# One layer of a post-norm decoder on one core: attention loads the turned x that the recurrence wrote to DRAM

## The chip, the core and the metric

The kernel runs on one core of a Trainium2 chip. The metric is the device time of one execution in microseconds (us). The core has a matrix engine (TensorE, PE in the profile, with its weight loads as PEld), VectorE (DVE), ScalarE (ACT), GpSimd (POOL) and SyncE (SP), which here issues every DMA. Engines run their own instruction streams in order and meet at semaphores.

## The reference, cut to what matters

Three layers follow each other, each with a residual and a layer norm behind it: a gated recurrence, a cross attention with `ctx_1024` as keys and values, and a quantised feed-forward. The batch is 64, the sequence 128, the width 256, with 16 heads of 16, all in float32.

```python
def _L0_attn_ref(x, Wq, Wk, Wv, Wf, bf, Wg, Wout, gamma, beta):
    q = (x @ Wq).reshape(b, s, H, HD)      # k and v alike
    fg = jax.nn.sigmoid(x @ Wf + bf).reshape(b, s, H, HD)
    ...
    def step(state, inp):
        qt, kt, vt, gt = inp
        state = state * gt[..., None] + vt[..., None] * kt[..., None, :]
        out_t = jnp.einsum('bhij,bhj->bhi', state, qt)
        return (state, out_t)
    ...
    out = (out - mu) * jax.lax.rsqrt(var + EPS) * gamma + beta
    out = out * jax.nn.silu(x @ Wg)
    return out @ Wout
...
x = _layernorm(x + _L0_attn_ref(x, ...), axis=-1)
x = _layernorm(x + _L0_xattn_ref(x, ctx_1024, ctx_1024, ...), axis=-1)
x = _layernorm(x + _L0_ffn_ref(x, ...), axis=-1)
```

x is a factor of two kinds of products: q, k, v and f of the recurrence, and the gate `x @ Wg`, which is computed later. Both need x with its features on the partitions, that is, x turned.

## The kernel before

The program is three blocks, one behind the other with a barrier between them: `recurrence_block` (L73), `attention_block` (L759) and `feedforward_block` (L1406). The first two work on pairs of batch rows, 32 pairs (`NP`) of 2 x 128 tokens. Despite its name the attention block also finishes the first layer: it loads the raw output of the recurrence, normalises it, multiplies it with the gate, applies `Wout`, adds x, and then does the cross attention.

**Recurrence.** Each engine runs a list of steps; in step p the front of pair p and the back of pair p-1 are done. SP's list is `load` (L196, the x of a pair: one DMA of 128 KB for the first batch row and four of 32 KB for the second, whose four chunks of 32 tokens are placed in reverse order) and `store` (L202, the output of a pair, one and four DMAs in the same way). Its loop (L232 to L236) runs over i = 2j+u: wait until pair i+1 has been turned, load pair i+3, wait until the output of pair i is ready, store pair i. An output is ready late: the back of pair i is done in step i+1, and its last sums, `total` on DVE (L712) and `gather` on POOL (L284), fall in step i+2. So `store(p-2)` is issued in the middle of step p, and `load(p+2)` directly behind it, since its own wait has long been met.

PE turns x with four transposes (`turn`, L326) into the PSUM bank F[0], and ACT copies the bank to `xT` (`turned`, L517). `xT` has one buffer of 128 x 2 x 256 float32 (256 KB). In step p, after the uses of exponent bank k = 1, ACT writes the turned x of pair p+1 (L547, L548); behind that copy on ACT stand the other uses of the exponents (L545), and PE waits for it in `value_gate(p+1, 0)` (L338), behind which stand the rest of the step's matmuls.

**Attention.** In a step PE, ACT, DVE and POOL work on four pairs at once (`old`, `prev`, `now`, `next_`). PE's order is written out in `step` (L1034). There x is loaded again from the input (`load`, L863), turned again by PE in `turn_x` (L912) through bank F[0] and copied by ACT in `x_out` (L1085) to the attention's own `xT`. Its reader is `gate` (L928). `turn_maxima` (L982) uses bank F[0] as well and therefore waits for the copy of x (`p.turned`), as does the first `turn_x1` (L946). The untransposed x in `xs` is needed for the residual too (L1299). The attention holds its batch rows in natural order.

**Feed-forward.** It is not touched.

Of the kernel before, what the change touches and what calls it, by code (L numbers as in the profile page):

```python
# [69 lines left out]

def recurrence_block(nc, t, w, x_d, o_d):  # L73

# [24 lines left out]
    with ExitStack() as ctx:  # L101
# [6 lines left out]
        def bank(name):  # L108
# [51 lines left out]

        loaded = [sem(f"rec_loaded{i}") for i in range(2)]
        stored = [sem(f"rec_stored{i}") for i in range(2)]
        names = """marked consts consts_ready x_made xT_ready vf_made v_ready z_ready ez_ready lg_ready h_ready n_ready q_made q_ready
            k_made k_ready e_made e_ready w_ready mt_made mt_ready o_made o_taken added out_ready seen""".split()
        q = {n: sem("rec_" + n) for n in names}
# [26 lines left out]
        with nc.Block() as block:  # L192

            @block.sync
            def _(sp):
                def load(pair, slot):  # L196
                    sp.dma_start(xs[:, slot, 0], x_d[bass.ds(2 * pair, 1)].rearrange("b t d -> (b t) d")).then_inc(loaded[slot], 16)
                    for chunk in range(NC):
                        sp.dma_start(xs[rows(place(1, chunk)), slot, 1],
                                     x_d[bass.ds(2 * pair + 1, 1), rows(chunk)].rearrange("b t d -> (b t) d")).then_inc(loaded[slot], 16)  # L200

                def store(pair, slot):  # L202
                    sp.wait_ge(q["out_ready"], pair + 1)
                    sp.dma_start(o_d[bass.ds(2 * pair, 1)].rearrange("b t d -> (b t) d"), o[:, slot, 0:D]).then_inc(stored[slot], 16)
                    for chunk in range(NC):
                        sp.dma_start(o_d[bass.ds(2 * pair + 1, 1), rows(chunk)].rearrange("b t d -> (b t) d"),
                                     o[rows(place(1, chunk)), slot, D:]).then_inc(stored[slot], 16)

                for s in range(2):
                    sp.sem_inc(stored[s], DMAS)  # L210
                load(0, 0)
                for i, name in ((2, "v"), (3, "f")):
                    sp.dma_start(t["w_rec"][:, :, i, :], w[name].rearrange("(c p) d -> p c d", p=P)).then_inc(qw["w_loaded"], 16)
                sp.dma_start(t["bf_row"][:], w["bf"].partition_broadcast(3)).then_inc(qw["bf_loaded"], 16)
                for i, name in ((0, "q"), (1, "k")):
                    sp.dma_start(t["w_rec"][:, :, i, :], w[name].rearrange("(c p) d -> p c d", p=P)).then_inc(qw["w_loaded"], 16)
                load(1, 1)
                sp.dma_start(t["raw_down"][:], w["down"].rearrange("(c p) d -> p c d", p=P)).then_inc(qw["raw_loaded"], 16)
                for i, name in enumerate(("up", "gate")):
                    sp.dma_start(t["raw_ff"][:, i], w[name].rearrange("(c p) d -> p c d", p=P)).then_inc(qw["raw_loaded"], 16)  # L220
                for i, name in enumerate(("xq", "xk", "xv", "xo")):
                    sp.dma_start(raw_x[:, i], w[name].rearrange("(c p) d -> p c d", p=P)).then_inc(qw["rest_loaded"], 16)
                for dst, src in (("w_g", "g"), ("w_out", "out")):
                    sp.dma_start(t[dst][:], w[src].rearrange("(c p) d -> p c d", p=P)).then_inc(qw["rest_loaded"], 16)
                for dst, src in (("gamma", "gamma"), ("beta", "beta"), ("bq", "bq"), ("bk", "bk")):
                    sp.dma_start(t[dst][:], w[src].rearrange("(c p) -> p c", p=P),
                                 allow_slow_non_contiguous=True).then_inc(qw["rest_loaded"], 16)
                for dst in ("bv", "bo"):
                    sp.dma_start(t[dst][:], w[dst].partition_broadcast(P)).then_inc(qw["rest_loaded"], 16)
                sp.wait_ge(q["x_made"], 1)  # L230
                load(2, 0)
                with sp.Fori(0, NP // 2 - 2) as j:  # L232
                    for u in range(2):
                        sp.wait_ge(q["x_made"], 2 * j + u + 2)
                        load(2 * j + 3 + u, 1 - u)
                        store(2 * j + u, u)  # L236
                sp.wait_ge(q["x_made"], NP - 2)
                load(NP - 1, 1)
                for p in range(NP - 4, NP):
                    store(p, p % 2)  # L240
                sp.wait_ge(qw["rest_loaded"], 16 * 12)
                for s in range(2):
                    sp.wait_ge(stored[s], DMAS + DMAS * NP // 2)
# [269 lines left out]
            def _(act):  # L513
# [2 lines left out]

                def turned(p):  # L517
                    act.wait_ge(q["x_made"], p + 1)
                    A.activation(xT.rearrange("p k n -> p (k n)"), F[0][:], ACT.Copy).then_inc(q["xT_ready"], 1)

                def step(p, s, before, front, back):
# [234 lines left out]

def attention_block(nc, t, x_d, ctx_d, o_d):  # L759

    NP = B // 2
    NR = 4
    with ExitStack() as ctx:
# [6 lines left out]
        def bank(name):  # L770
# [42 lines left out]
        own = th[:, 0:HH]  # L813
        qw = {n: sem("w_" + n) for n in "consts ready".split()}

        a_loaded = [sem(f"a_loaded{i}") for i in range(2)]
        names = """xT_made xT_ready cT_made cT_ready x1T_made x1T_ready q0_made q1_made q_ready zg_made th_ready sg_ready
            k_made k_ready on_ready onT_made ogb_ready y_ready v_made v_ready wout_made res1_ready x1_ready x1b_ready
            s_made s_taken m_ready mt_made mt_ready t_made e_ready pv_made ld_ready ls_ready rc_ready merged crossed seen
            att_ready wo_made res2_ready x2_ready var_o rstd_o var_1 rstd_1 var_2 rstd_2  # L820
# [3 lines left out]
        class Pair:  # L824
# [3 lines left out]

            def __init__(self, j, c):
                self.r, self.s, self.turn = 2 * j + c, c % 2, j + c // 2  # L830
                self.first = isinstance(j, int) and c == 0
                self.last = isinstance(j, int) and c == NP - 1
                self.turned = min(c + 3, NP) if isinstance(j, int) else 2 * j + (c + 3)

        def steps(eng, step):

# [22 lines left out]
        with nc.Block() as block:  # L859

            @block.sync
            def _(sp):
                def load(pair, slot):  # L863
                    two = bass.ds(2 * pair, 2)
                    for dst, src in ((xs, x_d), (cs, ctx_d), (os_, o_d)):
                        sp.dma_start(dst[:, slot], src[two].rearrange("b t d -> t b d")).then_inc(a_loaded[slot], 16)

                load(0, 0)
                load(1, 1)
                with sp.Fori(0, (NP - 2) // 2) as j:  # L870
                    for u in range(2):
                        sp.wait_ge(q["x1_ready"], 2 * (2 * j + 1 + u))
                        load(2 * j + 2 + u, u)

            @block.tensor
            def _(pe):
# [32 lines left out]
                                     start=(kc == 0), stop=(kc == KC - 1))  # L909
                    m.then_inc(done, 1)  # L910

                def turn_x(p):  # L912
                    pe.wait_ge(a_loaded[p.s], 48 * (p.turn + 1))
                    wait_if(pe, q["q_ready"], 4 * p.r - 6)
                    wait_if(pe, q["xT_ready"], p.r)
                    turn4(F[0], xs[:, p.s], q["xT_made"])

                def turn_context(p):
                    wait_if(pe, q["v_ready"], p.r)
                    pe.wait_ge(a_loaded[p.s], 48 * (p.turn + 1))  # L920
# [5 lines left out]
                    turn4(F[2], on, q["onT_made"])  # L926

                def gate(p):  # L928
                    pe.wait_ge(q["xT_ready"], p.r + 1)
                    pe.wait_ge(q["ogb_ready"], 2 * p.r + 2)  # L930
                    across(F[2], t["w_g"], xT, q["zg_made"])

# [11 lines left out]
                    along(F[1], cT, wx[:, 2], q["v_made"])  # L944

                def turn_x1(p):  # L946
                    if p.first:
                        pe.wait_ge(q["xT_ready"], p.r + 2)
                    else:
                        pe.wait_ge(q["mt_ready"], 2 * p.r - 1)  # L950
                    pe.wait_ge(q["x1_ready"], 2 * p.r + 2)
                    turn4(F[0], x1, q["x1T_made"])

# [28 lines left out]
                def turn_maxima(p, b):  # L982
# [5 lines left out]
                            pe.wait_ge(q["x1T_ready"], p.r + 2)  # L988
                    else:
                        pe.wait_ge(q["q_ready"], 4 * p.r + 2)  # L990
                        pe.wait_ge(q["xT_ready"], p.turned)
                    pe.wait_ge(q["m_ready"], n + 1)
                    T.transpose(MT, t["mparts"].rearrange("p a h -> p (a h)"), t["ident_b"][:]).then_inc(q["mt_made"], 1)

# [39 lines left out]
                def step(at):  # L1034
# [8 lines left out]
                        values(old, 1)  # L1043
                    if next_:
                        turn_o(next_)
                        turn_x(next_)
                    if now:
                        vals(now)
                    if prev:
# [29 lines left out]
            def _(act):  # L1079
                A = nc.scalar  # L1080

                def flat(ap):
                    return ap.rearrange("p k n -> p (k n)")

                def x_out(p):  # L1085
                    act.wait_ge(q["xT_made"], p.r + 1)
                    A.activation(flat(xT), F[0][:], ACT.Copy).then_inc(q["xT_ready"], 1)

                def context_out(p):
                    act.wait_ge(q["cT_made"], p.r + 1)  # L1090
# [54 lines left out]
                def step(at):  # L1145
# [6 lines left out]
                        A.preload_act_table_set("natural_log_exp_and_others")  # L1152
                    if old:
                        logs(old, 1)
                    if next_:
                        x_out(next_)
                    if old:
                        inverse(old, 1)
                    if next_:
# [887 lines left out]
def decoder_layer(nc, x_d, ctx_d, w, out_d):  # L2047

    with ExitStack() as ctx:
# [3 lines left out]
        NT = B * S // 512  # L2053
        stats_seen = ctx.enter_context(nc.semaphore("stats_seen"))
        o_d = nc.dram_tensor("rec_scratch", (B, S, D), F32).ap()
        r_d = nc.dram_tensor("raw_scratch", (NT, P, FC * 512), F32).ap()
        g_d = nc.dram_tensor("gate_scratch", (NT, P, FC * 512), F32).ap()
        u_d = nc.dram_tensor("product_scratch", (NT, P, FC * 512), F32).ap()
# [8 lines left out]
        with ExitStack() as early:  # L2067
# [13 lines left out]
                "v_half": se("v_half", [P, 2, 2, HH, 6 * HD]),  # L2081
                "raw_ff": se("raw_ff", [P, 2, FC, D]), "raw_down": se("raw_down", [P, KC, FF]),
            })
            recurrence_block(nc, t, w, x_d, o_d)
            attention_block(nc, t, x_d, ctx_d, o_d)
        feedforward_block(nc, t, r_d, g_d, u_d, out_d)


# [25 lines left out]
```

## Time and profile before

| | |
|---|---|
| median of 3 runs | 2022.22 us (2022.18 to 2028.58) |
| the profiled execution | 2018.74 us |
| its span, first to last instruction | 2016.6 us |
| PE / DVE / ACT / POOL busy | 92% / 79% / 61% / 19% |
| mean granted TensorE clock | 0.977 of full |
| DMA | 205.24 MB, mean 102 GB/s |

The recurrence takes the span from its start to about 755 us, the attention runs until about 1400 us, and the feed-forward takes the rest. The busy share of a whole span is a mean over three stages with different limits. For a change to single steps the timeline of a step is read: what each engine does at which time, how long it was idle ahead of an instruction, and who released it. The times of DMAs on SP's timeline are those of issuing them; from the start of the issue to the landing is a column of the DMA view.

### The profile page before, as it was taken

Reading aid. Unit: us, or ns where it says so; the run is one execution under the profiler, and the core shown is the slowest. Engines: PE = TensorE matmul, PEld = TensorE weight load, DVE = VectorE, ACT = ScalarE, POOL = GpSimd, SP = SyncE. Lnnn points to the kernel's source line nnn. Section 1 sums busy time; section 2 is a strip of 40 time slices with the busy share of each in tenths; the row PEclk is TensorE's granted clock in tenths of the full one; section 3 lists DMA queues with packets and bytes.
Section 4 is the critical chain, followed back from the end, with each engine's and each line's share of the span. In section 5 each row is a group of like instructions: output and inputs, shape, how many; then the busy total and the mean of one; then the engine's idle time right before and its main releaser. Section 6 shows DMA issues by size and latency. Waiting matters only on the chain. (4 is left out here: it accounts for less than half of the span.)

```text
span 2016.6 us, 71020 instructions
## 1 busy us (share of the span) xinstructions
PE 1864.5 (92%) x28151; PEld 1307.0 (65%) x28151; DVE 1593.3 (79%) x2870; ACT 1221.4 (61%) x2047; POOL 390.4 (19%) x516
## 2 busy tenths in 40 slices
PE   6999999999999977999999999999599988799798
PEld 4666666666666665888888888887344433344687
DVE  6777777777777775888888888887466799998897
ACT  4444554444445434777777777777355666688565
POOL 1111111211111121223232323232100222100121
PEclk9999999999999989999999999999699999999899
DMA  4001100110011001111111111110188788599574
GB/s 126 24 24 29 30 24 24 29 30 24 24 27 32 19 19 63 34 48 32 46 33 46 36 42 38 40 41 7 40 273 267 272 314 312 188 402 409 184 271 148
DMA packets 121324, 205.24 MB, mean 102 GB/s; under 512 B 44851, under 2 KB 98358, under 8 KB 121142
## 3 DMA queue, kind: packets, MB, share of 16 engines
q1 hardware_dynamic: 121142, 202.43, 29.4%
q8 instruction: 162, 2.65, 0.5%
q14 instruction: 20, 0.16, 0.0%
HBM read 108.01 MB, written 85.98 MB: 96 GB/s over the span
## 5 line engine op out<-in xcount | busy, mean ns | idle before, releaser
L1483 PE MATMUL ff_twin<-ff_xq,w_uh 128*128 (+1 forms) x1152 | 346.0, 382 | 40.0 <-DVE ff_top L1852 25.7
L1483 PEld LDWEIGHTS ff_twin<-ff_xq,w_uh 128*128 128x128 f16 x1152 | 110.4, 98 | 188.9 <-issue 43.2
L1483 PE MATMUL ff_twin<-ff_xq,w_ul 128*128 (+1 forms) x576 | 219.9, 382 | 0.0
L1214 DVE TENSOR_REDUCE mneg<-att_s 128x4 f32<-128x512 f32 x256 | 158.8, 683 | 31.3 <-PE att_s L977 31.3
L545 ACT ACTIVATE x<-rec_e,rec_hidden 128x512 f32<-128x512 f32 x256 | 155.8, 702 | 35.1 <-PE rec_e L380 35.1
L661 DVE TENSOR_TENSOR x<-rec_x,rec_until 128x512 f32<-128x512 f32 x256 | 158.7, 681 | 17.2 <-PE rec_x L364 17.2
L392 PE MATMUL rec_x<-x 32*32 32x64 f32 x8192 | 146.4, 219 | 14.9 <-DVE x L661 9.5
L392 PEld LDWEIGHTS rec_x<-x 32*32 32x32 f32 x8192 | 125.4, 107 | 51.4 <-issue 51.3
L288 POOL TENSOR_TENSOR rec_o<-rec_tmp 128x512 f32<-128x512 f32 x32 | 41.1, 1283 | 571.6 <-DVE rec_tmp L714 571.6
L1129 ACT ACTIVATE att_e<-att_s 128x512 f32<-128x512 f32 x256 | 132.2, 612 | 25.4 <-PE att_s L1011 25.4
L349 PE MATMUL rec_f<-rec_xT,w_rec 128*128 128x256 f32 x512 | 137.3, 402 | 0.8 <-ACT rec_v L527 0.8
L341 PE MATMUL rec_f<-w_rec,rec_xT 128*128 128x512 f32 x256 | 128.8, 626 | 6.2 <-DVEq L594 5.0
L697 DVE TENSOR_TENSOR rec_tmp<-rec_x,x 32x256 f32<-32x256 f32 (+1 forms) x192 | 80.8, 421 | 66.8 <-PE rec_x L420 49.1
L691 DVE TENSOR_TENSOR rec_tmp<-rec_x,x 128x512 f32<-128x512 f32 x128 | 83.9, 682 | 56.8 <-PE rec_x L392 56.8
L1913 DVE TENSOR_TENSOR ff_out<-ff_whole,s_other 128x1536 f32<-128x1536 int16 x64 | 111.9, 1755 | 17.1 <-ACT s_other L1670 13.3
L349 PEld LDWEIGHTS rec_f<-rec_xT,w_rec 128*128 128x128 f32 x512 | 90.5, 191 | 32.9 <-ACT rec_v L527 11.2
L1917 DVE TENSOR_REDUCE ff_topg<-ff_out 128x1536 f32 (+1 forms) x64 | 109.9, 1739 | 0.2 <-DVE ff_coef L1900 0.2
L545 ACT ACTIVATE x<-rec_e 128x512 f32<-128x512 f32 x64 | 38.1, 597 | 118.4 <-PE rec_e L380 118.4
L684 DVE TENSOR_TENSOR x<-x,rec_v 128x2048 f32<-128x2048 f32 x32 | 73.4, 2292 | 43.7 <-ACT x L545 43.7
L1137 ACT ACTIVATE att_ld<-att_a,part 128x256 f32<-128x256 f32 x128 | 65.2, 560 | 63.6 <-PE att_a L1023 63.2
L1862 DVE TENSOR_REDUCE ff_top<-ff_out 128x1536 f32 (+1 forms) x32 | 56.1, 1754 | 58.7 <-ACT ff_out L1619 58.7
L1483 PEld LDWEIGHTS ff_twin<-ff_xq,w_ul 128*128 128x128 f16 x576 | 56.5, 98 | 67.6 <-issue 1.7
(244 smaller groups left out, 4363.3 us busy)
## 6 DMA issues: line engine op xcount, KB each, us to landing
raw_scratch<-ff_out SPq DMA_DIRECT2D x32, 768.0 KB, 3.5
ff_in<-raw_scratch SPq DMA_DIRECT2D x32, 768.0 KB, 5.9
gate_scratch<-ff_out SPq DMA_DIRECT2D x28, 768.0 KB, 3.5
ff_in<-gate_scratch SPq DMA_DIRECT2D x28, 768.0 KB, 10.2
product_scratch<-ff_out SPq DMA_DIRECT2D x28, 768.0 KB, 9.7
ff_out<-product_scratch SPq DMA_DIRECT2D x28, 768.0 KB, 5.9
att_x<-in_x SPq DMA_DIRECT2D x32, 256.0 KB, 2.7
att_ctx<-in_ctx SPq DMA_DIRECT2D x32, 256.0 KB, 3.0
```

The costliest lines, as they stand in the source:

```text
L341: T.matmul(bank_[:], xT[:, kc, b * P:(b + 1) * P], wr[:, kc, 2:4].rearrange("p a d -> p (a d)"), start=(kc == 0), stop=False)
L349: m = T.matmul(bank_[:, oc * 2 * P:(oc + 1) * 2 * P], wr[:, kc, i, oc * P:(oc + 1) * P], xT[:, kc], start=(kc == 0), stop=(kc == KC - 1))
L392: m = T.matmul(X[k][rows(c), h * NR * HD:(h + 1) * NR * HD].rearrange("p (r i) -> p r i", r=NR), mt[rows(c), b, hd, rows(c)], e[rows(c), s ...
L545: A.activation(out, E[(s + k) % 2][:], ACT.Exp, bias=hidden[:, asks, r:r + 1] if r < NR else 0.0, scale=-1.0 if asks else 1.0).then_inc(q[ ...
L661: V.tensor_tensor(mt[:, b].rearrange("p (a j m) n -> p j a m n", a=KC, m=2)[:, j], X[j].rearrange("p (a m n) -> p a m n", a=KC, m=2), unti ...
L691: V.tensor_tensor(tmp[:, k * HH:(k + 1) * HH, 0:NR], X[k].rearrange("p (h r i) -> p h r i", r=NR, i=HD), um[:, s, :, k * HH * HD:(k + 1) * ...
L697: V.tensor_tensor(tmp[lanes, b * H:(b + 1) * H, k], bank_[lanes, b * D:(b + 1) * D].rearrange("p (h i) -> p h i", i=HD), e[lanes, s, k, b ...
L1129: A.activation(e[:, b, j], X[j][:], ACT.Exp).then_inc(q["e_ready"], 1)
L1214: V.tensor_reduce(mneg[:, 4 * j:4 * j + 4], X[j].rearrange("p (h k) -> p h k", h=4), AX.X, ALU.max, negate=True).then_inc(q["s_taken"], 1)
L1483: m = T.matmul(bank_.rearrange("p (b n) -> p b n", b=BT), weights(wp, kc, a, c), tile[:, xp, :, kc], start=(i == 0), stop=(i == len(terms) ...
L1913: V.tensor_tensor(ob[:, u, s], whole[:, u, s], other[:, s], ALU.mult).then_inc(q["prod"], 1)
L1917: V.tensor_reduce(topg[:, bass.ds(2 * k + s, 1)], ob[:, u, s], AX.X, ALU.max, apply_absolute_value=True).then_inc(q["maxed"], 1)
```

## The change

In the recurrence SP stores each pair's `xT` to a DRAM tensor of 32 x 256 KB (`store_turned`, one DMA). The store of pair i+1 stands between `load(i+3)` and `store(i)` in the loop. Since `xT` has one buffer, ACT waits before each copy until the store of the pair before has landed (`xT_stored`). In the attention PE no longer turns x and ACT no longer copies it; `turn_x`, `x_out` and the waits that guarded the bank go. Instead SP loads the turned x of a pair with five DMAs on one semaphore (`load_turned`): one for the first batch row, in runs of 512 bytes, and four for the second, in runs of 128 bytes, which put the four chunks in natural order. SP issues them when the gate product of the pair before has been made (`zg_made`), since this `xT` has one buffer as well. The gate waits for that load.

```diff
@@ recurrence_block, SP
+                def store_turned(pair):
+                    sp.wait_ge(q["xT_ready"], pair + 1)
+                    sp.dma_start(xt_d[bass.ds(pair, 1)].rearrange("b p n -> (b p) n"),
+                                 xT.rearrange("p k n -> p (k n)")).then_inc(xT_stored, 16)
...
                 sp.wait_ge(q["x_made"], 1)
                 load(2, 0)
+                store_turned(0)
                 with sp.Fori(0, NP // 2 - 2) as j:
                     for u in range(2):
                         sp.wait_ge(q["x_made"], 2 * j + u + 2)
                         load(2 * j + 3 + u, 1 - u)
+                        store_turned(2 * j + u + 1)
                         store(2 * j + u, u)
                 sp.wait_ge(q["x_made"], NP - 2)
                 load(NP - 1, 1)
                 for p in range(NP - 4, NP):
+                    if p < NP - 1:
+                        store_turned(p + 1)
                     store(p, p % 2)
+                sp.wait_ge(xT_stored, 16 * NP)
@@ recurrence_block, ACT
                 def turned(p):
                     act.wait_ge(q["x_made"], p + 1)
+                    wait_if(act, xT_stored, 16 * p)
                     A.activation(xT.rearrange("p k n -> p (k n)"), F[0][:], ACT.Copy).then_inc(q["xT_ready"], 1)
@@ attention_block, SP
+                def load_turned(pair):
+                    one = bass.ds(pair, 1)
+                    src = xt_d[one].rearrange("b p (k n) -> (b p) k n", k=KC)
+                    sp.dma_start(xT[:, :, 0:P], src[:, :, 0:P]).then_inc(xT_loaded, 16)
+                    for chunk in range(NR):
+                        at, place = P + chunk * P // NR, P + (NR - 1 - chunk) * P // NR
+                        sp.dma_start(xT[:, :, at:at + P // NR], src[:, :, place:place + P // NR]).then_inc(xT_loaded, 16)
+
                 load(0, 0)
+                load_turned(0)
                 load(1, 1)
+                sp.wait_ge(q["zg_made"], 1)
+                load_turned(1)
                 with sp.Fori(0, (NP - 2) // 2) as j:
                     for u in range(2):
                         sp.wait_ge(q["x1_ready"], 2 * (2 * j + 1 + u))
                         load(2 * j + 2 + u, u)
+                        sp.wait_ge(q["zg_made"], 2 * j + 2 + u)
+                        load_turned(2 * j + 2 + u)
@@ attention_block, PE and ACT
-                def turn_x(p):
-                    pe.wait_ge(a_loaded[p.s], 48 * (p.turn + 1))
-                    wait_if(pe, q["q_ready"], 4 * p.r - 6)
-                    wait_if(pe, q["xT_ready"], p.r)
-                    turn4(F[0], xs[:, p.s], q["xT_made"])
...
                 def gate(p):
-                    pe.wait_ge(q["xT_ready"], p.r + 1)
+                    pe.wait_ge(xT_loaded, 16 * (1 + NR) * (p.r + 1))
...
                         pe.wait_ge(q["q_ready"], 4 * p.r + 2)
-                        pe.wait_ge(q["xT_ready"], p.turned)
...
                     if next_:
                         turn_o(next_)
-                        turn_x(next_)
...
-                def x_out(p):
-                    act.wait_ge(q["xT_made"], p.r + 1)
-                    A.activation(flat(xT), F[0][:], ACT.Copy).then_inc(q["xT_ready"], 1)
...
-                    if next_:
-                        x_out(next_)
```

## Rows read from the trace of the kernel before

**Rows 1.** Busy time by stretch: stretch, length, then PE, PEld, DVE, ACT, POOL
```profile
1000.00:1200.00 200.00, 200.00 (x2560) 164.48 (x2552) 176.50 (x469) 154.85 (x300) 60.88 (x110) 1.00 0.12 38
```

**Rows 2.** Timeline of SP, one recurrence step: start, length, line, DMA, count
```profile
399.40 0.37 SPq L204 DMA_DIRECT2D rec_scratch<-rec_o  x1
...
403.32 0.37 SPq L197 DMA_DIRECT2D rec_x<-in_x  x1
403.89 3.07 SPq L199 DMA_DIRECT2D rec_x<-in_x  x4
```

**Rows 3.** Timelines of POOL and ACT in the same step
```profile
397.96 1.26 POOL L290 TENSOR_TENSOR rec_o<-rec_o,rec_tmp 128x512 f32<-128x512 f32 x1
...
404.39 0.63 ACT L519 ACTIVATE rec_xT<-rec_f 128x512 f32<-128x512 f32 x1
```

**Rows 4.** Timelines of PE and DVE around the copy of turned x, same step
```profile
404.42 1.11 PE L407 MATMUL rec_x<-rec_wa,x 64*64 64x16 f32 x32
405.46 1.98 PE L341 MATMUL rec_f<-w_rec,rec_xT 128*128 128x512 f32 x4
...
406.21 2.29 DVE L684 TENSOR_TENSOR x<-x,rec_v 128x2048 f32<-128x2048 f32 x1 [1.50 <-ACT x L545]
```

**Rows 5.** SP's last load issue and ACT's copy, steps 2 and 29
```profile
66.44 2.47 SPq L199 DMA_DIRECT2D rec_x<-in_x  x4
...
67.50 0.63 ACT L519 ACTIVATE rec_xT<-rec_f 128x512 f32<-128x512 f32 x1
...
673.17 2.93 SPq L199 DMA_DIRECT2D rec_x<-in_x  x4
...
674.08 0.63 ACT L519 ACTIVATE rec_xT<-rec_f 128x512 f32<-128x512 f32 x1
```

**Rows 6.** DMA issues: queue, kind, count, KB each, median us to landing
```profile
raw_scratch<-ff_out SPq DMA_DIRECT2D x32, 768.0 KB, 3.5
...
att_x<-in_x SPq DMA_DIRECT2D x32, 256.0 KB, 2.7
...
rec_scratch<-rec_o SPq DMA_DIRECT2D x32, 128.0 KB, 1.8
```

**Rows 7.** Timeline of PE in two recurrence steps that stalled, without L380
```profile
173.31 1.09 PE L392 MATMUL rec_x<-x 32*32 32x64 f32 x64 [1.81 <-DVE x L661]
174.33 1.13 PE L349 MATMUL rec_f<-rec_xT,w_rec 128*128 128x256 f32 x4
...
577.47 1.09 PE L392 MATMUL rec_x<-x 32*32 32x64 f32 x64 [1.99 <-DVE x L661]
578.49 2.08 PE L349 MATMUL rec_f<-rec_xT,w_rec 128*128 128x256 f32 x4
580.50 1.72 PE L392 MATMUL rec_x<-x 32*32 32x64 f32 x64
```

**Rows 8.** Busy time by stretch; the number third from the end is the clock
```profile
578.00:579.00 1.00, 1.00 (x42) 0.90 (x32) 1.00 (x2) 0.00 (x0) 0.00 (x0) 0.72 0.38 128
...
742.00:743.00 1.00, 0.00 (x0) 0.00 (x0) 0.00 (x0) 0.00 (x0) 0.00 (x0) 0.64 0.00 0
```

**Rows 9.** Timelines of PE, ACT and PEld in one attention step
```profile
1012.42 0.60 PE L885 MATMUL att_f<-ident,att_x 128*128 128x128 f32 x4
1012.85 1.89 PE L901 MATMUL att_f<-w_x,att_cT 128*128 128x256 f32 x8
...
1013.92 0.42 ACT L1143 ACTIVATE att_ld<-att_ld 128x256 f32<-128x256 f32 x1 [0.27 <-POOL att_ld L1378]
...
1015.14 0.27 ACT L1124 ACTIVATE mT<-att_f 128x128 bf16<-128x128 bf16 x1
...
1015.49 0.44 PEld L1011 LDWEIGHTS att_s<-mT,pick_b 32*128 32x128 bf16 x16
```

**Rows 10.** Timeline of PE: the gate product of two steps running
```profile
1000.24 2.00 PE L893 MATMUL att_f<-att_xT,w_g 128*128 128x256 f32 x8
...
1020.33 2.00 PE L893 MATMUL att_f<-att_xT,w_g 128*128 128x256 f32 x8
```

More of the change, by code:

```diff
@@ L69, in wait_if, with recurrence_block @@
         eng.wait_ge(sem, value)
-def recurrence_block(nc, t, w, x_d, o_d):
+def recurrence_block(nc, t, w, x_d, o_d, xt_d):
     NP = B // 2
@@ L754, in _, with attention_block @@
                 weights()
-def attention_block(nc, t, x_d, ctx_d, o_d):
+def attention_block(nc, t, x_d, ctx_d, o_d, xt_d):
     NP = B // 2
@@ L814, in attention_block @@
         qw = {n: sem("w_" + n) for n in "consts ready".split()}
+        xT_loaded = sem("a_xT_loaded")
         a_loaded = [sem(f"a_loaded{i}") for i in range(2)]
-        names = """xT_made xT_ready cT_made cT_ready x1T_made x1T_ready q0_made q1_made q_ready zg_made th_ready sg_ready
+        names = """cT_made cT_ready x1T_made x1T_ready q0_made q1_made q_ready zg_made th_ready sg_ready
             k_made k_ready on_ready onT_made ogb_ready y_ready v_made v_ready wout_made res1_ready x1_ready x1b_ready
@@ L830, in __init__ @@
                 self.r, self.s, self.turn = 2 * j + c, c % 2, j + c // 2
-                self.first = isinstance(j, int) and c == 0
                 self.last = isinstance(j, int) and c == NP - 1
-                self.turned = min(c + 3, NP) if isinstance(j, int) else 2 * j + (c + 3)
         def steps(eng, step):
@@ L946, in turn_x1 @@
                 def turn_x1(p):
[L947 to L950, printed above, removed]
+                    wait_if(pe, q["mt_ready"], 2 * p.r - 1)
                     pe.wait_ge(q["x1_ready"], 2 * p.r + 2)
@@ L2055, in decoder_layer @@
         o_d = nc.dram_tensor("rec_scratch", (B, S, D), F32).ap()
+        xt_d = nc.dram_tensor("turned_scratch", (B // 2, P, KC * 2 * P), F32).ap()
         r_d = nc.dram_tensor("raw_scratch", (NT, P, FC * 512), F32).ap()
@@ L2083, in decoder_layer @@
             })
-            recurrence_block(nc, t, w, x_d, o_d)
-            attention_block(nc, t, x_d, ctx_d, o_d)
+            recurrence_block(nc, t, w, x_d, o_d, xt_d)
+            attention_block(nc, t, x_d, ctx_d, o_d, xt_d)
         feedforward_block(nc, t, r_d, g_d, u_d, out_d)
```

1 line of the change is left out of this document (added).

## The prediction

> **What bounds the kernel now.** I read the page's busy slices first, then the busy time by stretch, and then the timelines of one step in each stage that the change touches. In the middle of the attention PE is busy for the whole 200 us of the stretch at full clock, DVE for 176.5, ACT for 154.9 [rows 1]. So PE's order sets the attention's time, unless a chain through another engine is just as long; the timeline has to tell. In the recurrence no engine is full: the order written out between PE, DVE and ACT sets it, at (674.08 - 67.50)/27 = 22.5 us a step on average [rows 5]. SP issues its DMAs in bursts and is mostly idle. That makes it look free, but the question is when in a step its bursts fall, and for that SP's timeline stands beside those of POOL and ACT.
>
> In the step shown, POOL finishes the output of pair p-2 at 397.96 + 1.26 = 399.22 [rows 3], SP starts its store at 399.40 and ends issuing the load behind it at 403.89 + 3.07 = 406.96 [rows 2]: ten DMAs, 7.6 us. ACT copies the turned x at 404.39 [rows 3], in the middle of SP's burst. PE starts the product that needs this copy at 405.46, with only 0.44 us between the copy's end (404.39 + 0.63 = 405.02) and that start [rows 3, 4].
>
> **Part 1: the store of the turned x and ACT's new wait.** In SP's program the store of xT for pair p stands behind `store(p-2)` and `load(p+2)`, and `store(p-2)` waits for POOL in step p. ACT's copy of pair p+1, also in step p, now waits until exactly this store has landed. The chain of a step is therefore: POOL's output, ten issues on SP, the eleventh, its landing, ACT's copy, `value_gate` on PE. Behind ACT's wait are queued two uses of the exponents (L545), for which DVE's weighting waits (its idle time of 1.50 us ended with that very L545) [rows 4]; behind PE's are the rest of the border products, the next step's scores, and so DVE's `total` and POOL's next output. Nothing of the next burst can start earlier, so the stall comes back in every step and is not worked off.
>
> Its size, term by term:
> - From ACT's copy, as it stands today, to the end of SP's last issue. Taken from both timelines for all steps from 2 to 29, 28 of them: 66.44 + 2.47 - 67.50 = 1.41 us in the first, 673.17 + 2.93 - 674.08 = 2.02 us in the last [rows 5], 2.57 in the step of the other rows [rows 2, 3]. The mean of the 28 is 1.08 us, since in four of them a late PE delays the copy as well (two of these four are shown [rows 7]); those delays are thereby counted as cover.
> - To the start of the eleventh issue: 0.20 us, as between a first and a second DMA (403.32 + 0.37 to 403.89) [rows 2].
> - From its issue to its landing. No row shows a write of 256 KB from SBUF. Writes of 128 KB landed in 1.8 us and of 768 KB in 3.5 [rows 6]; on the line between them 256 KB take 1.8 + 1.7 x 128/640 = 2.14 us. Bounds are 1.8 and the 2.7 of a load of 256 KB in shorter runs [rows 6]. I take 2.14, since it is the same direction and the same queue.
> - The release of ACT: some 0.1 us (POOL's end at 399.22 to SP's start at 399.40 is 0.18 [rows 2, 3]; 0.08 from 1015.14 + 0.27 to PE's weight load at 1015.49 [rows 9]).
>
> The copy is late by 1.08 + 0.20 + 2.14 + 0.10 = 3.52 us. PE has 0.44 - 0.08 = 0.36 us of slack there, so the step grows by 3.16 us: 28 x 3.16 = 88.5 us. Bounds from the landing alone: 28 x 2.82 = 79 and 28 x 3.72 = 104. Steps 0, 1 and 30 don't have a store and a load ahead of the eleventh issue at once; I give them 0 to 1 us in all and take 0.5.
>
> The Trainium skill, "DMA: Bandwidth & Descriptors", section "Anatomy of one DMA", gives about 2.0 us fixed, mostly the wait for the write receipt, and bytes over 436 GB/s on top. By that page the landing would be 2.6 us, an estimate, and the sum 13 us higher; the shortest writes here landed in less than its fixed part, so the trace is below the page. The sum does not use it.
>
> **Part 2: TensorE's clock.** The stall is an idle time of PE of about 3.2 us, once per step, where today it is nearly full. The recurrence shows what shorter ones do. Four steps have an idle time of 1.8 to 2.0 us on PE. After one of 1.81 us the next four L349 took the normal 1.13 us; after one of 1.99 us they took 2.08, and the L392 behind them 1.72 instead of 1.09 [rows 7]: the granted clock fell to the lower level, 1.2 GHz, while they ran (0.72 in that microsecond) [rows 8]. It fell in two of the four. Near the block's end it also fell in a longer idle time (0.64 in a microsecond with PE at rest) [rows 8]. One fall costs (2.08 - 1.13) + (1.72 - 1.09) = 1.58 us [rows 7]. With 3.2 us idle I expect it in nearly every step, and the dense products of `value_gate` stand right behind it: 28 x 1.58 = 44 us. Bounds: 0 if the clock holds, and twice the price (88) if it stays low for twice as long.
>
> **Part 3: what goes from the attention.** PE's four transposes have the slot from 1012.42 to 1012.85, 0.43 us [rows 9], once a pair: 32 x 0.43 = 13.8 us if only PE counted. ACT's copy of x (0.60 us) stood in ACT's wait for POOL: the next instruction was idle for another 0.27 us until POOL released it [rows 9]. So ACT's chain through logs, POOL's sum, inverse and o keeps its time, and ends with the copy of the turned maxima at 1015.14 + 0.27 = 1015.41. PE's weight load that needs it starts at 1015.49, 0.08 us later [rows 9]. An earlier PE finds that input not ready: the slot becomes waiting time at the shift. I count 2 us for the whole stage, from its first steps, where PE isn't full; bounds 0 and 13.8.
>
> **Part 4: the attention's new load.** SP issues it after the gate product of the pair before and it is needed for the next one: 1002.24 to 1020.33, 18 us [rows 10]. Five issues at 0.57 to 0.77 us each [rows 2] are about 4 us, and even 768 KB landed in 3.5 us [rows 6]. Hidden, cost 0. Its runs of 128 bytes have no row of their own; it would take over 14 us to land before the gate waits. SP's next load comes behind `zg_made`, but that load waits for the next x1 anyway. The DMAs add 8.4 MB written and 8.4 MB read beside PE-bound work: 0.
>
> **Sum.** Against the profiled execution: 2018.7 + 88.5 + 44 + 0.5 - 2 = 2149.7 us. The median of the runs lies 3.5 us above that execution (2022.22 to 2018.74), so the forecast is 2153 us, 6.5% slower.
>
> **Rivals.**
> 1. *The stall without the clock.* An idle time of about 3 us a step, but PE's density around it keeps the clock high, as after two of the four idle times. 2153 - 44 = 2109 us. For: short products before the gap are dense enough today. Against: every idle time over 2 us near the block's end did lower it.
> 2. *A longer low clock or a later landing.* The clock stays low for twice as long (44 more: 2197), and with the store landing in 2.7 us (16 more) it is 2213 us.
> 3. *Faster: PE sets the attention, and the store is in time.* It needs the copy to be late by less than 0.36 + 0.43 = 0.8 us a step, that is, an xT store issued ahead of the output's store. Then the 13.8 us of transposes decide: 2022 - 14 = 2008 us. For: PE is busy for the whole stretch [rows 1]. Against: SP's burst lies where rows 2 put it, and the program order forbids the earlier issue. A balance within 0.3% needs stall and gain to cancel.
> 4. *The load of 128-byte runs is late.* If it takes 2 us more than the 18, each of 32 gates waits: 64 us on top, 2217 us. The Trainium skill, "DMA: Bandwidth & Descriptors", section "Why small descriptors are slow (HBM only)", says that each short run carries a fixed overhead; that speaks against the chunked load, and no row here prices it.
>
> **How the numbers follow.** Forecast 0.55, rival 1 0.20, rival 2 0.15, rival 4 0.03, rival 3 0.05, a balance within 0.3% 0.02. A measurement of this kernel can tell about 0.3% (6 us) from no change. So faster 0.05, same 0.02, slower 0.93. The range goes from 2095 (rival 1 with half of the attention's slot and a landing of 1.8 us) to 2205 (most of rival 2).
>
> **What the profile after would show.** In recurrence steps 2 to 29 ACT's L519 is idle before it, released by the DMA of the turned scratch, and starts 8.5 to 9 us after the start of the output's store instead of 5; PE has an idle time of about 3 us ahead of the first L341 of a step; the step takes about 27 us instead of 22.5 (22.5 + 3.16 + 1.58); the granted clock in the recurrence is near 0.93. In the attention the step stays near 20.09 us and PE shows a wait for mT ahead of L1011. I am wrong if L519 isn't released by a DMA, if the clock stays at 1.00, or if the attention's step falls to 19.7 us.

## The result, and the profile after

| | before | after |
|---|---|---|
| median of the runs shown together | 2023.55 us (4 runs) | 2195.27 us (4 runs) |
| the profiled execution | 2018.74 us | 2192.99 us |
| its span | 2016.6 us | 2190.9 us |
| mean granted TensorE clock | 0.977 | 0.931 |

The changed kernel takes 1.082 times as long (95% interval 1.077 to 1.0876). It moves 222.03 MB instead of 205.24. Ratios and intervals here and below are of fast runs alone: one of these four runs after (2217.22 us), one of e5's four, one of e7's twelve and one of the kernel before beside e1 to e4 were in a slower state.

Nearly all of the loss is in the recurrence. Split by the first issue of the attention's loads and by the first and last start of the score products, the two profiled spans differ like this: recurrence 755.0 to 933.8 us (+178.8), from there to the first scores (L977, now L992) 34.1 to 35.3 (+1.2), the scores from first to last 632.5 to 628.0 (-4.5), the rest 595.0 to 593.8 (-1.2); in sum +174.3 us.

**One recurrence step.** The timeline of SP after the change (start, length, line, DMA, count) shows the burst of ten issues and the eleventh, the store of the turned x, behind it. It answers [rows 2].

```profile
403.93 0.37 SPq L205 DMA_DIRECT2D rec_scratch<-rec_o  x1
404.50 2.33 SPq L207 DMA_DIRECT2D rec_scratch<-rec_o  x4
407.12 0.37 SPq L198 DMA_DIRECT2D rec_x<-in_x  x1
407.69 2.73 SPq L200 DMA_DIRECT2D rec_x<-in_x  x4
410.61 0.37 SPq L212 DMA_DIRECT2D turned_scratch<-rec_xT  x1
```

The timelines of ACT, PE and DVE in the same step (the idle time before an instruction and its releaser stand in brackets) answer [rows 3, 4]:

```profile
412.72 0.60 ACT L531 ACTIVATE rec_xT<-rec_f 128x512 f32<-128x512 f32 x1 [3.64 <-DMA turned_scratch<-rec_xT]
...
408.97 1.11 PE L418 MATMUL rec_x<-rec_wa,x 64*64 64x16 f32 x32
413.37 3.78 PE L352 MATMUL rec_f<-w_rec,rec_xT 128*128 128x512 f32 x4 [3.29 <-ACT rec_xT L531]
...
414.51 2.29 DVE L696 TENSOR_TENSOR x<-x,rec_v 128x2048 f32<-128x2048 f32 x1 [5.25 <-ACT x L557]
```

ACT's copy (L531, once L519) starts 412.72 - 403.93 = 8.79 us after the output's store; before the change that was 404.39 - 399.40 = 4.99 us. PE is idle for 3.29 us where it had none, and the product behind the idle time takes 3.78 us instead of 1.98. DVE then waits 5.25 us for the exponents instead of 1.50. The waits of the stretch from 60 to 840 us (total us, times, longest) say that this is the pattern of nearly every step:

```profile
DVE x L696 <- ACT x L557: 140.7, 27, 6.9
ACT rec_xT L531 <- DMA turned_scratch<-rec_xT: 104.0, 27, 5.5
...
PE rec_f L352 <- ACT rec_xT L531: 87.4, 26, 4.6
```

From the copy of step 1 to that of step 29 a step takes (851.85 - 46.13)/28 = 28.78 us on average, against (674.08 - 45.66)/28 = 22.44 between the same two copies before: 6.33 us more (from the unrounded means).

**The clock.** Busy time by stretch (PE, PEld, DVE, ACT, POOL; third from the end the granted clock). The first two rows are long stretches of the recurrence in the kernel before, the next two are the same stretches after the change, and the others follow one idle time of PE.

```profile
60.00:400.00 340.00, 322.67 (x8071) 226.53 (x8074) 253.66 (x366) 164.67 (x286) 62.77 (x47) 0.99 0.10 26
400.00:700.00 300.00, 285.21 (x7126) 200.26 (x7115) 222.55 (x318) 147.32 (x256) 37.60 (x29) 0.99 0.10 27
...
60.00:400.00 340.00, 287.43 (x6355) 192.49 (x6358) 199.65 (x289) 132.38 (x228) 48.37 (x36) 0.87 0.11 30
400.00:700.00 300.00, 251.81 (x5300) 165.65 (x5292) 166.46 (x241) 109.82 (x191) 34.41 (x26) 0.84 0.10 29
...
412.00:416.00 4.00, 2.63 (x3) 1.18 (x4) 1.49 (x1) 1.75 (x3) 0.00 (x0) 0.51 0.06 21
416.00:420.00 4.00, 4.00 (x39) 2.32 (x37) 1.42 (x3) 0.00 (x0) 0.00 (x0) 0.50 0.00 0
420.00:424.00 4.00, 4.00 (x135) 2.82 (x134) 0.93 (x3) 1.20 (x2) 0.00 (x0) 0.50 0.02 4
424.00:428.00 4.00, 4.00 (x24) 1.93 (x23) 2.22 (x6) 1.28 (x3) 0.00 (x0) 0.78 0.00 0
```

The clock stays at the lower level, 1.2 GHz, for 13.7 us, from 412.1 to 425.8, while PE is busy all the time from 413.37 on. Two groups of the page carry the same news: the value and gate products now take 859 ns each, where the page of before has 626, and the idle time ahead of DVE's weighting has grown from 43.7 to 152.8 us.

```profile
L352 PE MATMUL rec_f<-w_rec,rec_xT 128*128 128x512 f32 x256 | 184.0, 859 | 98.1 <-ACT rec_xT L531 93.0
...
L696 DVE TENSOR_TENSOR x<-x,rec_v 128x2048 f32<-128x2048 f32 x32 | 73.4, 2292 | 152.8 <-ACT x L557 152.8
```

**Attention.** The middle of the stage by stretch, which answers [rows 1]:

```profile
1000.00:1200.00 200.00, 199.96 (x2542) 163.26 (x2541) 177.52 (x471) 149.66 (x292) 61.05 (x110) 1.00 0.20 53
```

The timelines of PE and SP: the gate product of two steps running, as [rows 10], and between them SP's issues of the new load.

```profile
1198.94 1.99 PE L917 MATMUL att_f<-att_xT,w_g 128*128 128x256 f32 x8
...
1201.09 0.57 SPq L882 DMA_DIRECT2D att_xT<-turned_scratch  x1
1201.85 2.72 SPq L885 DMA_DIRECT2D att_xT<-turned_scratch  x4
...
1218.93 1.99 PE L917 MATMUL att_f<-att_xT,w_g 128*128 128x256 f32 x8
```

One of the waits of the stretch from 1000 to 1200 us (total us, times, longest):

```profile
PEld att_f L1007 <- DVE mparts L1227: 3.2, 9, 0.4
```

The step takes 1218.93 - 1198.94 = 19.99 us instead of 20.09. The new load is issued right behind the gate product; its last issue ends at 1201.85 + 2.72 = 1204.57, 14 us before the next gate product. PE now waits for DVE at the turning of the maxima, which is a wait that the kernel before did not have.

### The profile page after: what moved, and what is told of

It reads as the page before. It is cut to its first block and busy times, and to the rows that moved or that the text cites. A ratio compares the mean times of both kernels' runs of the same rounds, so it can differ in the third digit from the quotient of the medians.

```text
span 2190.9 us, 71227 instructions
## 1 busy us (share of the span) xinstructions
PE 1945.4 (89%) x28023; PEld 1332.8 (61%) x28023; DVE 1594.2 (73%) x2870; ACT 1208.4 (55%) x2015; POOL 390.4 (18%) x516
## 2 busy tenths in 40 slices
DMA packets 169452, 222.03 MB, mean 101 GB/s; under 512 B 80691, under 2 KB 142390, under 8 KB 169270
## 3 DMA queue, kind: packets, MB, share of 16 engines
q8 instruction: 162, 2.65, 0.5%
## 5 line engine op out<-in xcount | busy, mean ns | idle before, releaser
L352 PE MATMUL rec_f<-w_rec,rec_xT 128*128 128x512 f32 x256 | 184.0, 859 | 98.1 <-ACT rec_xT L531 93.0
L696 DVE TENSOR_TENSOR x<-x,rec_v 128x2048 f32<-128x2048 f32 x32 | 73.4, 2292 | 152.8 <-ACT x L557 152.8
L557 ACT ACTIVATE x<-rec_e,rec_hidden 128x512 f32<-128x512 f32 x256 | 155.0, 695 | 34.1 <-PE rec_e L391 32.1
L352 PEld LDWEIGHTS rec_f<-w_rec,rec_xT 128*128 128x128 f32 x256 | 60.5, 261 | 153.4 <-ACT rec_xT L531 94.6
```

Source lines behind the costliest of these rows:

```text
L352: T.matmul(bank_[:], xT[:, kc, b * P:(b + 1) * P], wr[:, kc, 2:4].rearrange("p a d -> p (a d)"), start=(kc == 0), stop=False)
L557: A.activation(out, E[(s + k) % 2][:], ACT.Exp, bias=hidden[:, asks, r:r + 1] if r < NR else 0.0, scale=-1.0 if asks else 1.0).then_inc(q[ ...
```

## The experiments

The line numbers of ACT's copy, PE's products and so on shift by one or two between the kernels. The kernel before ran beside each group of experiments: 2025.7 us median beside e1 to e4, 2023.66 beside e5 to e8.

### e1_order: the store of xT one step earlier

```diff
-                        store_turned(2 * j + u + 1)
+                        store_turned(2 * j + u + 2)
                         store(2 * j + u, u)
```

With `store_turned(1)` ahead of the loop. SP has then issued the store of a pair's turned x long before it waits for POOL in the next step.

> Edit: SP stores xT of pair i+2 instead of pair i+1 ahead of store(i), so that each store of xT goes out right after its copy, in the step before, and not behind the ten issues that wait for POOL. Theory A (the whole loss in the recurrence comes from the place of this store in SP's order, and the slow clock from the idle time that it makes): ACT's copy no longer waits for a DMA, the recurrence step is back at 22.5 us and the clock at its upper level there, 2020 us (2014 to 2028), some 3 us of it gained in the attention (0.10 us a step). Theory B (the extra 256 KB write and the wait for it cost by themselves, wherever they stand): 2100 us or more.

Measured: 2018.96 us median, 0.997 of before (0.9957 to 0.9983). In the recurrence ACT's copy no longer waits for any DMA. Its step around 400 us, SP and then ACT:

```profile
400.44 0.37 SPq L205 DMA_DIRECT2D rec_scratch<-rec_o  x1
401.01 2.81 SPq L207 DMA_DIRECT2D rec_scratch<-rec_o  x4
404.45 0.37 SPq L198 DMA_DIRECT2D rec_x<-in_x  x1
405.02 2.55 SPq L200 DMA_DIRECT2D rec_x<-in_x  x4
407.75 0.37 SPq L212 DMA_DIRECT2D turned_scratch<-rec_xT  x1
...
405.42 0.63 ACT L532 ACTIVATE rec_xT<-rec_f 128x512 f32<-128x512 f32 x1
```

The copy is again 4.98 us behind the output's store (4.99 before the change), and the eleventh issue, which follows it, stores the pair just copied. So 176 us hang on which pair the eleventh issue serves. The DMAs, their number, the 16.8 MB and the whole change of the attention are still there; none of these costs anything that shows. The gain of 0.3% is clear of the noise, and the attention accounts for most of it (the scores take 627.9 us instead of 632.5).

### e6_two_buffers: the wait taken away by a second buffer

SP's order is that of the changed kernel. Only `xT` in the recurrence has two buffers, so that ACT waits for the store of two pairs before.

```diff
-                xT = sb("rec_xT", [P, KC, 2 * P])
+                xT = sb("rec_xT", [P, 2, KC, 2 * P])
...
-                def turned(p):
+                def turned(p, s, before):
                     act.wait_ge(q["x_made"], p + 1)
-                    wait_if(act, xT_stored, 16 * p)
+                    wait_if(act, xT_stored[s], 16 * before)
```

> Edit: the changed kernel with two buffers of xT in the recurrence and SP's order as it is; ACT's copy of pair p+1 waits for the store of pair p-1, which SP issued in the step before. Theory A (the wait is for the one buffer, made late by the order): the wait goes, as with the store one step earlier, 2019 us (2013 to 2028). Theory B (eleven issues of SP behind each other, or the added writes, hold something else up): 2040 us or more.

Measured: 2015.76 us, 0.9967 (0.9955 to 0.998). SP, then ACT, in its step around 400 us:

```profile
401.35 0.37 SPq L205 DMA_DIRECT2D rec_scratch<-rec_o  x1
...
408.62 0.37 SPq L212 DMA_DIRECT2D turned_scratch<-rec_xT  x1
...
406.34 0.63 ACT L532 ACTIVATE rec_xT<-rec_f 128x512 f32<-128x512 f32 x1
```

The copy starts 4.99 us behind the output's store and does not wait. The same burst with the same eleventh store behind it costs nothing once no engine waits for it. This and e1 settle the wait as the cause, by two ways that share no edit.

### e3_ahead_of_load: the store of xT ahead of the load

```diff
-                        load(2 * j + 3 + u, 1 - u)
                         store_turned(2 * j + u + 1)
+                        load(2 * j + 3 + u, 1 - u)
                         store(2 * j + u, u)
```

It still comes behind the output's store of the step, so five of the ten issues stand ahead of it.

> Edit: in SP's loop the store of xT stands ahead of the load instead of behind it; it is still behind store(i), which waits for POOL. That takes five of the ten issues (3.3 us) out of the chain. Theory A (the wait is the sum of the issues ahead plus the landing): the copy would be late by 2.9 + 0.2 + 2.3 + 0.1 - 5.0 = 0.5 us instead of 3.9, nearly all inside PE's slack of 0.4 us; the clock stays up; 2025 us (2018 to 2040). Theory B (what counts is the write's landing, not its place behind the load): the wait stays above 2 us and the time above 2120 us.

Measured: 2049.5 us, 1.0138 (1.0109 to 1.0166), above the expected range. The waits from 60 to 700 us have this line left of the big one:

```profile
ACT rec_xT L532 <- DMA turned_scratch<-rec_xT: 23.1, 21, 2.2
```

The copy comes 6.5 us behind the output's store on average (9.5 in the changed kernel), a step takes 23.51 us, 1.07 more than before. Moving the store ahead of half the burst takes away 146 of the 172 us. The expectation was 25 us too low: from the issue to the copy it took 3.1 us on average instead of the 2.3 + 0.1 expected, which is the landing (below), and between 60 and 700 us the clock was at its lower level nine times, where it was twice before.

### e4_store_only: the recurrence as changed, the attention as before

Edit: the whole attention block is the one of the kernel before; the turned x is written and never read.

> Edit: the recurrence of the changed kernel with the attention of the kernel before, which turns x itself; the stored xT is written and not read. Theory A: the recurrence is as long as in the changed kernel, the attention step is back at 20.09 us from 19.99, together 2193 + 3 = 2196 us (2180 to 2215). If the removed transposes had brought their whole slot of 0.43 us a pair, this run would be 14 us above the changed kernel, 2207 us, with an attention step 0.43 us longer than there.

Measured: 2204.69 us in one run. The scores extend over 631.5 us, as before (632.5), where the changed kernel has 628.0. The attention's step is 20.09 us, as before. So the new load and the lost transposes are worth some 3 to 5 us together, and the loss is all in the store and its wait. The total is 12 us above the changed kernel's execution, nearer to the 2207 us at which the transposes would have been worth their whole slot; but 7 of these 12 us lie in the recurrence (940.9 us instead of 933.8), which is the same code in both, and one run does not give its scatter.

### e2_filler and e5_filler3: PE kept busy during the wait

Ahead of PE's wait for the turned x stand five (e2) or three (e5) more products per step into a bank that is free; their result is used by nobody. The wait remains, but PE is not idle in it.

```diff
                         wait_if(pe, q["q_ready"], 2 * p)
+                        for _ in range(3):
+                            T.matmul(F[1][:], ident[:], wr[:, 0, 2:4].rearrange("p a d -> p (a d)"), start=True, stop=True)
```

> Edit: the changed kernel, with five extra matmuls of 128 x 512 float32 (0.5 us each at full clock) ahead of PE's wait for the copy in value_gate, into the bank that value_gate overwrites; their result is not used. Theory A (of the 6.25 us that a recurrence step has grown, about 3.2 are the wait itself and 3.0 the lower clock that the idle time brings): the clock stays up, the steps fall by about 3 us each, 2193 - 28 x 3 = 2109 us (2100 to 2130). Theory C (the growth beyond the wait is a later landing or a longer chain through DVE and not the clock): no gain, 2190 us or more, as the extra matmuls only add work.

> Edit: as the filler before, with three extra matmul calls instead of five. The five took 4.5 us in the trace and not 2.5, since each call is two instructions of 0.455 us, and so were longer than the wait that they were to fill; a step took 4.5 us more than in the kernel before, with the clock up. Three take 2.7 us, less than the wait of 3.4 to 3.9. Theory A (beyond the wait the growth is the clock): the step is 22.5 + 3.6 us, 2019 + 28 x 3.6 - 3 = 2117 us (2105 to 2135). Theory C (the clock is not what costs): 2180 us or more.

Measured: e2 2162.75 us (1.0686, 1.0663 to 1.071), e5 2143.42 us (1.0596, 1.0574 to 1.0618). Both do strictly more work than the changed kernel and are 33 and 52 us faster. The clock by stretch in e5:

```profile
60.00:400.00 340.00, 310.51 (x6804) 204.40 (x6804) 214.09 (x307) 142.24 (x245) 52.42 (x39) 0.99 0.11 33
400.00:700.00 300.00, 275.44 (x6092) 182.52 (x6089) 189.74 (x276) 124.83 (x216) 35.46 (x27) 0.99 0.11 32
```

and one step of it, the added products on PE first:

```profile
393.18 2.84 PE L350 MATMUL rec_f<-w_rec,ident 128*128 128x512 f32 x6
...
397.03 0.60 ACT L533 ACTIVATE rec_xT<-rec_f 128x512 f32<-128x512 f32 x1 [5.20 <-DMA turned_scratch<-rec_xT]
...
397.68 1.98 PE L354 MATMUL rec_f<-w_rec,rec_xT 128*128 128x512 f32 x4 [1.65 <-ACT rec_xT L533]
```

ACT still waits, even longer than in the changed kernel (4.0 us on average, 3.9 there), but the clock is back at 0.99 and the product at 1.98 us. This shows that the lower clock is a price of its own, and that it goes when PE's idle time is filled (ahead of the product 0.8 us of it are left in a step on average, against 3.2 in the changed kernel). Both missed their expectations. For e2 a call of the added product turned out to be two instructions of 0.46 us, so the five took 4.56 us, longer than the wait in 25 of 27 steps, and set the step themselves. For e5 they took 2.8 us and PE still waited in 20 of 27 steps (1.0 us there), so its step of (793.03 - 48.80)/28 = 26.58 us is nearly the step with the stall alone: 26.58 - 22.44 = 4.1 us of stall, where its expectation had 3.6 and the prediction 3.16. In the other seven steps the added products themselves may hold PE, so 4.1 is an upper bound.

### e7_order_act and e8_before_act: the wait for mT in the attention

e7 is e1 with one swap in ACT's order; e8 is the kernel before with the same swap.

```diff
-                    if next_:
-                        o_out(next_)
                     if prev:
                         shift_out(prev, 0)
-                        exps(prev, 0)
+                    if next_:
+                        o_out(next_)
+                    if prev:
+                        exps(prev, 0)
```

> Edit: the store of xT one step earlier, as in the run with that edit alone, and in the attention ACT copies the turned maxima of the first half (mT) ahead of its two instructions on o instead of behind them. Theory A (the removed transposes gave only 0.10 us a step because PE then waits for mT and for DVE's maxima): mT comes up to 0.8 us earlier, PE's wait for it goes and only that for the maxima stays, 0.1 to 0.3 us a step, 2013 us (2008 to 2017) where the edit of the store alone gave 2019. Theory D (DVE's maxima alone hold PE): no difference, 2019 us.

> Edit: the kernel before with ACT's order in the attention changed in the same way, x turned by PE as before. Theory A: there PE's own order sets the shift (its weight load starts 0.08 us behind mT, at the end of the loads ahead of it), so an earlier mT brings 0 to 2 us, 2023 us. If it brings as much as in the other run, the two edits don't depend on each other.

Measured: e7 2016.75 us, 0.9966 (0.9954 to 0.9979); e8 2023.78 us, 0.9998 (0.9986 to 1.001). e7 isn't told apart from e1 (0.997); its 2016.75 us lies in the range of theory A too, so the steps have to decide. Yet the swap did what it should. The timelines of ACT and PE in one step of e7:

```profile
1015.90 0.28 ACT L1134 ACTIVATE mT<-att_f 128x128 bf16<-128x128 bf16 x1 [0.18 <-PE att_f L1008]
...
1015.63 0.23 PE L1008 MATMUL att_f<-ident_b,mparts 128*128 128x128 bf16 x1
```

The same of e1, with the two groups of PE behind the turning:

```profile
1016.80 0.27 ACT L1134 ACTIVATE mT<-att_f 128x128 bf16<-128x128 bf16 x1
...
1015.91 0.23 PE L1008 MATMUL att_f<-ident_b,mparts 128*128 128x128 bf16 x1
1016.07 1.38 PE L1017 MATMUL att_s<-att_qm,att_kT 32*128 32x256 f32 x16
1017.12 0.55 PE L1026 MATMUL att_s<-mT,pick_b 32*128 32x128 bf16 x16
```

In e7 the turned maxima `mT` are copied 0.27 us behind the turning, in e1 0.89 us. The attention's step is 19.98 us in both. So the wait for `mT` that I had named does not hold the step. In e1 the turning of the maxima comes 14.02 us into a step against 14.34 before, so 0.32 of the 0.43 us of transposes are gained there, up to the point where PE waits for DVE's `mparts`. Then PE needs 1.69 us from the start of the turning to the start of the product behind the shift instead of 1.45, and 0.24 us are lost again, in e7 as in e1. In the stage's first two steps of full length and in its last that second loss is absent, and the step is 19.87 us, with the turning at 14.11. The single instructions show where it arises. In those three steps, and before the change in all but one, the first four of the sixteen products of L1017 (once L1002) start within 0.02 us of each other; in all the other steps of e1 and e7 their starts are spread over 0.26 us, the rest follow them, and the group takes 1.38 us instead of 1.15. Why the four start apart was not found; the granted clock is 1.00 there.

## Why the prediction was right, and where its terms were off

The prediction was 2153 us in a range of 2095 to 2205, and 2195 came out, in the upper part of the range. The mechanism and its place were right, two terms were too small, and both in the same direction.

- **The eleventh issue behind the burst, ACT released by it: right.** ACT's copy waits for `turned_scratch` in all 28 steps from 2 to 29. Taking the wait away in two ways (e1, e6) brings the loss to nothing.
- **How late the copy comes: 3.52 us predicted, 4.1 measured.** It starts 9.50 us behind the output's store on average over steps 3 to 29 and 5.41 before (the four late steps of [rows 7] are in that mean). The term that failed is the landing: 2.14 + 0.10 us from issue to copy was predicted, 2.78 is the mean. In 14 of the 27 steps it is 2.1 to 2.25, as on the line through [rows 6]; in eleven 3.3 to 4.1, and in two between. The other terms of the sum held: up to the eleventh issue it came to 9.50 - 2.78 = 6.72 us, where they give 5.41 + 1.08 + 0.20 = 6.69. The 2.6 us that the prediction estimated from the Trainium skill, "DMA: Bandwidth & Descriptors", section "Anatomy of one DMA", are nearer to the mean. But the page gives its figures for DMAs that GpSimd issues, these are SP's, and the trace shows two groups with hardly a store at 2.6.
- **The stall: 3.16 us a step predicted, 3.7 to 4.1.** 9.50 - 5.41 - 0.36 = 3.73 from the trace of the changed kernel, at most 4.1 from e5, where more stores landed late (3.13 us from issue to copy). Over 28 steps that is 104 to 115 us instead of 88.5.
- **The clock: 44 us predicted, 62 to 73.** The rest of the 6.33 us: 2.2 to 2.6 us a step. I had taken one fall to cost 1.58 us, from the one step of [rows 7], in which the clock was low for 3.4 us. In the changed kernel there are 28 stretches of low clock in these steps, 215 us in sum: 17 last 3.4 or 6.8 us and one 10.2, but ten last 13.7 us, as the one from 412 to 426. The time from the copy of a step to the next copy is 27.4 us on average where a stretch of 3.4 us followed the stall, and 31.5 where one of 13.7 did. Against a step with the stall alone, 22.44 + 3.73 = 26.17 us, that is an estimate of 1.2 and 5.3 us for a fall. So the price of 1.58 held for a short stretch, and the step of the prediction that failed is that every fall would be a short one. The bound of twice the price covered it.
- **The signs: the clock's was missed.** The recurrence was to be near 0.93 and was at 0.87 and 0.84; 0.931 is the mean of the whole execution. The step was to take about 27 us and took 28.78, and the copy was to start 8.5 to 9 us behind the output's store and started at 9.50.
- **Rival 1 (no fall of the clock): fell**, by the stretches above; e2 and e5 are what it looks like. **Rival 2 (a longer low clock, a later landing): this is what came**, 2195 beside its 2197 to 2213, both of its causes in part. One fall, seen once, had carried the whole price; that was too little for 0.55 against 0.15.
- **The attention: right in size, wrong in its link.** 2 us predicted, 3 to 5 measured; the signs said that PE would wait for `mT` ahead of the shift. In e1 the copy of `mT` does end only 0.05 us before the shift starts (16.80 + 0.27 to 17.12), but e7 shows that this is not what holds the step. DVE's maxima are one link ahead, and behind them the late starts within L1017, whose cause is open.
- **The new load: right, cost 0.** Its 32 KB parts in runs of 128 bytes landed in 2.2 us, the 128 KB part in 2.5, over 12 us before they were needed. The Trainium skill, "DMA: Bandwidth & Descriptors", section "Why small descriptors are slow (HBM only)", speaks of an overhead for each short run. The trace is compatible with a small one: loads of 32 KB and 128 KB in the recurrence, whose runs are longer (1024 bytes), landed in 1.8 and 2.4 us, but they ran in another stage beside other DMAs, so the runs are not shown to be the reason. Rival 4 fell.
- **Rival 3 (faster, if the store were in time): its condition was right, its size not.** e1 meets the condition and gains 0.3% (6.7 us), not the 14 us of all transposes.

The sum with the measured terms: 28 x 6.33 = 177.3 us in the recurrence's steps, 1.5 in the rest of that stage, 1.2 up to the first scores, -4.5 in the scores and -1.2 behind them are the 174.3 us between the two spans.

## What to carry to other kernels

The DMA added here cost what its place in the queue made of it, not what it moved: ask what the issue waits behind, and whether anyone waits for its landing. Here one step's difference in which pair the same instruction stores, or a second buffer, turned a loss of 8% into a gain of 0.3% (both beat the kernel before). And where a wait opens an idle time on TensorE, count the clock as a second term with a range of its own: a single fall seen in a trace is one draw, and here the price went from about 1.2 to 5.3 us. Filling that time with useless products took 52 us off.

## What the runs showed of the hardware that was not expected

**A small store lands late where instruction packets pass at the same time.** The queue of instruction packets (162 packets, 2.65 MB, so 16 KB each) appears in the page beside the kernel's own, as a share of the same 16 engines. The page of the changed kernel:

```profile
q8 instruction: 162, 2.65, 0.5%
...
turned_scratch<-rec_xT SPq DMA_DIRECT2D x32, 256.0 KB, 2.3
```

The records of single packets, for the stores of the turned x of pairs 1 to 30 in five kernels, from the start of its first packet to that of its last (us), split by whether an instruction packet was under way in that time:

```
kernel                no instruction packet     with one
                      stores   median           stores   median
changed               18       0.75             12       2.20
e1_order              10       0.74             20       1.92
e3_ahead_of_load      13       0.76             17       1.84
e5_filler3            11       0.74             19       2.10
e6_two_buffers         7       0.75             23       2.02
```

In all 59 stores of the left group it is 0.9 us or less. A store that takes longer also has more time to meet such a packet, so the split was made again by the first 0.74 us of each store alone: 60 of the 63 without such a packet in that time take 0.9 us or less, and all 87 with one take 1.15 us or more. That the fetch delays the store is read from this coincidence; no run took the fetches away, so it isn't shown by experiment. What it means is that a median landing of a trace in which nobody waits for the DMA doesn't bound the landing on a critical path.

**A low clock can outlast its cause by far, and not by the length of the cause.** Behind an idle time of 3.3 us PE was busy from 413.37 us on without a gap, and the clock stayed at the lower level until 425.8 (rows above). In the kernel before the two such stretches in steps 2 to 29 lasted 3.4 us each; only in the last steps of the recurrence, from 725 us on, where PE had idle times of 2.0 to 2.5 us close behind each other, did one last 10.2 us. In the changed kernel the length of the idle time does not set it: behind an idle time of 4.42 us the clock was low for 3.4 us, behind one of 3.03 for 13.7. What goes with the length is where the fall lies against the end of the idle time. Of the 25 stalls of 2.9 us and more, ten had the fall 0.7 to 2.1 us ahead of that end, and the clock was low for 13.7 us; three had it 2.5 to 3.1 us ahead, and it was low for 6.8; eleven had it at most 0.5 us ahead or up to 0.6 us behind, and it was low for 3.4 us; the last had it 0.85 us behind, with 10.2 us. The 26 stalls of 2.5 us and more in e4 fall into the same groups. These runs do not show why.
